# A delta-rule layer on Trainium2: half of the output projection done in two parts, around the state inputs

## What is computed

```python
def _L0_attn_a_ref(x, Wq, Wk, Wv, Wbeta, Wg1, Wg2, g_norm, Wo):
    h, hd = (Wbeta.shape[0], d // Wbeta.shape[0])        # 16 heads of 32
    q = silu(x @ Wq.T).reshape(b, n, h, hd)
    k = silu(x @ Wk.T).reshape(b, n, h, hd)
    v = (x @ Wv.T).reshape(b, n, h, hd)
    beta = 2.0 * jax.nn.sigmoid(x @ Wbeta.T)
    k = k * jax.lax.rsqrt(jnp.sum(k * k, axis=-1, keepdims=True) + EPS)
    o = _delta_rule(q, k, v, beta).reshape(b, n, d)      # S += k (beta (v - k S)); o = q S
    gate = jax.nn.sigmoid(x @ Wg1.T @ Wg2.T)
    og = (o * gate).reshape(b, n, h, hd)
    rms = jax.lax.rsqrt(jnp.mean(og * og, axis=-1, keepdims=True) + EPS)
    og = (og * rms).reshape(b, n, d) * g_norm
    return og @ Wo.T
x = x + _L0_attn_a_ref(_layernorm(x, axis=-1), ...)
```

## Time and profile before

| | us |
|---|---|
| median of 3 runs | 5043.79 |
| lowest, highest | 5043.69, 5046.62 |
| span of the profiled execution | 5045.7 |

### The profile page before, as it was taken

The page is one execution under the profiler, slowest core; times in us unless marked ns, Lnnn a source line. Parts: engine busy times, 40 slices in busy tenths (PEclk is TensorE's granted clock), DMA queues, the critical chain, the costliest instruction groups (busy, mean ns, idle before and its releaser), DMA issues.

```text
span 5045.7 us, 144755 instructions
## 1 busy us (share of the span) xinstructions
PE 4586.8 (91%) x63104; PEld 3211.9 (64%) x63104; DVE 3631.5 (72%) x7890; ACT 2410.3 (48%) x4592; POOL 716.4 (14%) x909
## 2 busy tenths in 40 slices
PE   5799999999999998499999999999999999999998
PEld 4677777777777776356546646655654664665564
DVE  3677666676776666287787788778778778877876
ACT  3244433333333333164564565466456457546545
POOL 0000000000000000012211211221221221122121
PEclk9899999999999998699999999999999999999999
DMA  2222222222222222100000000000000000000000
GB/s 62 49 70 69 72 62 62 62 62 62 62 69 63 62 66 62 64 1 18 2 18 18 18 2 18 18 1 18 18 2 18 18 10 10 18 18 2 18 9 10
DMA packets 352135, 171.77 MB, mean 34 GB/s; under 512 B 300016, under 2 KB 300784, under 8 KB 350736
## 3 DMA queue, kind: packets, MB, share of 16 engines
q1 hardware_dynamic: 342528, 145.20, 10.8%
q10 hardware_dynamic: 8976, 17.30, 1.2%
HBM read 93.74 MB, written 67.63 MB: 32 GB/s over the span
## 4 chain that ended last, share of the span: by engine, by line
PE 43%; DVE 11%; ACT 2%; issue 1%; DMA 1%; POOL 1%; SPq 0%; DVEq 0%; ACTq 0%; POOLq 0%
PE row_psum L1682 9%; PE row_psum L1707 9%; PE row_psum L40 5%; PE row_psum L42 5%; PE row_psum L41 5%; DVE smax L1963 5%; PE row_psum L1695 4%; PE row_psum L1755 1%; DVE xr_lo L1831 1%; PE row_psum L1735 1%; DVE probs L1943 1%; PE row_psum L1473 1%; DVE stats L1797 1%; POOL rstd L1276 1%; PE row_psum L1654 1%
## 5 line engine op out<-in xcount | busy, mean ns | idle before, releaser
L1963 DVE TENSOR_REDUCE smax<-row_psum 128x1 f32<-128x512 f32 x2048 | 1270.4, 681 | 96.9 <-PE row_psum L1682 93.3
L1405 ACT ACTIVATE probs<-row_psum 128x512 f32<-128x512 f32 x2048 | 1090.7, 603 | 349.8 <-PE row_psum L1695 329.7
L1682 PE MATMUL row_psum<-k_stack,q_stack 64*128 64x512 f32 (+1 forms) x2048 | 740.3, 440 | 50.6 <-DVE smax L1963 24.5
L1695 PE MATMUL row_psum<-q_stack,k_stack 64*128 64x512 f32 (+1 forms) x2048 | 733.1, 458 | 22.3 <-ACT probs L1405 9.1
L1682 PEld LDWEIGHTS row_psum<-k_stack,q_stack 64*128 64x128 f32 (+1 forms) x2048 | 354.3, 188 | 499.5 <-DVE smax L1963 367.7
L1707 PE MATMUL row_psum<-probs,v_aug 128*32 128x512 f32 x4096 | 538.9, 603 | 1.6 <-ACT av_sb L1421 0.4
L1695 PEld LDWEIGHTS row_psum<-q_stack,k_stack 64*128 64x128 f32 (+1 forms) x2048 | 319.3, 184 | 225.8 <-ACT probs L1405 156.0
L876 DVE TENSOR_TENSOR lane_t<-lane_t,lane_p 128x30 f32<-128x30 f32 (+14 forms) x960 | 318.3, 332 | 33.0
L40 PE MATMUL row_psum<-wf_hi,xr_hi 128*128 128x320 f32 (+1 forms) x1024 | 331.9, 324 | 3.2 <-DVE xr_lo L1831 3.2
L873 DVE TENSOR_TENSOR lane_p<-lane_t 128x30 f32<-128x30 f32 (+14 forms) x960 | 315.5, 329 | 23.5
L42 PE MATMUL row_psum<-wf_hi,xr_lo 128*128 128x320 f32 (+1 forms) x1024 | 318.9, 311 | 0.0
(11 more groups left out here) (215 smaller groups left out, 10123.8 us busy)
## 6 DMA issues: line engine op xcount, KB each, us to landing
x_sp<-in_x ACTq DMA_DIRECT2D x33, 512.0 KB, 4.0
tri_dram<-tri SPq DMA_DIRECT2D x256, 64.0 KB, 2.0
lane_t<-tri_dram SPq DMA_DIRECT2D x32, 512.0 KB, 4.6
inv_dram<-lane_t SPq DMA_DIRECT2D x32, 512.0 KB, 2.6
inv_b<-inv_dram SPq DMA_DIRECT2D x256, 64.0 KB, 2.3
x_res<-in_x SPq DMA_DIRECT2D x32, 512.0 KB, 3.8
x<-x_res SPq DMA_DIRECT2D x32, 512.0 KB, 3.7
xs<-x SPq DMA_DIRECT2D x16, 1024.0 KB, 5.6
```

Source lines behind the costliest of these rows:

```text
L1405: act.activation(probs[:, h % PROBS, tt, :], ps[:, m % STACK_BANKS, :], ACT.Exp, scale=float(DH) ** -0.5).then_inc(exp_ready, 1)
L1682: pe.matmul(ps[:, bank, :], q_stack[rows, qt, P * st:P * st + P], k_stack[rows, kv, :], start=True, stop=True).then_inc(max_mm, 1)
L1695: pe.matmul(ps[:, m % STACK_BANKS, :], k_stack[rows, kv, P * tt:P * tt + P], q_stack[rows, qt, :], start=True, stop=True).then_inc(score_m ...
L1963: dve.tensor_reduce(smax[:, g, st:st + 1], ps[:, bank_of("max", NT * g + st), :], AX.X, ALU.max).then_inc(max_ready, 1)
```

## The change

`output` gets an argument, the input blocks that it is to go through. Its waits are made on the first of them, and the projection is reported as done (`wo_mm`) after the last. TensorE calls it for the second tile with the first two input blocks before `state_inputs` and with the other two after. Both parts add up in bank BB. VectorE's `add_residual` for that tile moves from before the portion "inputs" of the inversion to behind `advance(0)`.

```diff
-            def output(b, s, t, further, ahead):
-
-                if further:
+            def output(b, s, t, further, ahead, inputs=range(KT)):
+
+                if further and inputs[0] == 0:
...
-                pe.wait_ge(ohi_ready, at(b, s, TS, t + 1))
-                pe.wait_ge(olo_ready, at(b, s, TS, t + 1))
-                for k in range(KT):
+                if inputs[0] == 0:
+                    pe.wait_ge(ohi_ready, at(b, s, TS, t + 1))
+                    pe.wait_ge(olo_ready, at(b, s, TS, t + 1))
+                for k in inputs:
...
-                last.then_inc(wo_mm, 1)
+                if inputs[-1] == KT - 1:
+                    last.then_inc(wo_mm, 1)
...
                 without_state(*now)
                 if behind:
-                    output(*behind, 1, further, ahead)
+                    output(*behind, 1, further, ahead, range(KT // 2))
                 state_inputs(*now)
+                if behind:
+                    output(*behind, 1, further, ahead, range(KT // 2, KT))
                 chain(*now, 0)
...
                 invert_ahead("transitions")
+                invert_ahead("inputs")
+                advance(*now, 0)
                 if behind:
                     add_residual(*behind, 1)
-                invert_ahead("inputs")
-                advance(*now, 0)
                 invert_ahead("chain0")
```

## The result

| | before | changed |
|---|---|---|
| median us (runs) | 5045.2 (4) | 5008.7 (4) |
| lowest, highest | 5043.69, 5057.3 | 5002.86, 5017.61 |
| span of the profiled execution | 5045.7 | 5008.0 |
| mean granted TensorE clock over the span | 0.963 | 0.973 |

The ratio is 0.9924 [0.9906, 0.9941], so the kernel became 0.8% faster, where 0.4% was forecast (5023 us; 5008.7 lies within 5003 to 5049). A second set of runs of the changed kernel gave 5004.06 us (6 runs) beside 5043.86 for the kernel before (21 runs), ratio 0.9924 [0.99, 0.9949].

What follows compares the result with a forecast made beforehand. TensorE was taken to be bound in the state chain by waits for 256-instruction program blocks. From the 5045.7 us span, +6 switches, -15 blocks, -12 clock gave 5024.7, with the span 1.9 above the median 5023 us; range 5003 to 5049.

Steps and rivals of the forecast that it cites:

- Blocks, -15 us: TensorE's program blocks: large matmuls moved to the next block cut stalls by about 0.5 us a step, over 31 steps.
- Step A: Step kind whose chain stall of 1.52 us goes while one of about 1.0 us appears in state_inputs: gain 0.5 us.
- Step B: Step kind with a 1.90 us stall inside the chain: gain between 0.05 and 1.05 us, in the middle 0.55.
- floor of 3.85 us: Least time from edge to edge assumed for a 256-instruction TensorE block that ends in a stall.
- Switches, +6 us: One more pair of switches between large and tiny matmuls on TensorE: +0.2 us a step, bounds 0 and +11.
- The clock, -12 us: TensorE's granted clock: a quarter of the lower-clock time goes, at 0.35 us per microsecond; bounds 0 and -25 us.
- VectorE's move worth nothing itself: An earlier state add on VectorE gains nothing, since TensorE's own key sums set the start of chain 1.
- cover of 0.9 us for 0.69: VectorE's slack before the second state add, 0.9 us, hides the moved 0.69 us add, so it costs nothing.
- (1): Rival: the stall only moves between blocks and the clock is untouched; median 5042 us, chance 0.27.
- the Trainium skill's rule: Block edges in TensorE's instruction fetch are mostly hidden, so only the switch term remains: 5050 us, chance 0.05.
- (2): Rival: TensorE's clock falls earlier, ahead of the chain; slower, 5056 to 5065 us for ten such steps, chance 0.09.
- (3): Rival: VectorE's slack before the second state add goes; 5052 us, chance 0.04.

Runs made afterwards that it cites:

- 0 / 4: The changed kernel with all twelve matmuls of the second projection behind state_inputs, none ahead: 5073.39 us, ratio 1.0057 to the kernel before.
- three-and-one split: The changed kernel with nine of the twelve projection matmuls ahead of state_inputs and three behind: 5019.97 us, ratio 0.9953 to the kernel before.
- VectorE's part alone: The kernel before with only VectorE's add_residual moved behind advance(0), TensorE's order unchanged: 5037.19 us, ratio 0.998.
- tiny filler: The changed kernel with 64 extra unused tiny matmuls (128 in the trace) behind state_inputs in 29 of 32 steps: 5138.41 us, ratio 1.0193.

## Why the prediction came out as it did

**What bounds the kernel there** was read rightly. The stalls in the chain are edges of program blocks: a block of tiny matmuls put in stalls once a step, large ones without use take stalls away, 3.84 and 3.85 us between edges came back in two other kernels, and nearly every stall ends 1.15 to 1.6 us behind a packet of the instruction queue.

**Blocks, -15 us.** All rows of issue fell by 15.1 us. The split was as forecast as well: 20.9 us left before L693 and L699 (about 20 forecast), and 14.2 before L682; with the rows of L40 to L42, 5.3 us for all large matmuls of these lines, that makes at most 19.5 (15 to 20 forecast). Step by step it was less good. Step A stalls 0.85 us in L682 (forecast 1.0) and not at all in the chain (forecast none), so it gained 1.52 - 0.85 = 0.67 us there (0.5 forecast), less 0.29 for a longer stall before L672 (0.71 for 0.42). Step B gained 1.90 - 0.45 = 1.45 us, above the 1.05 of the upper end: the block ahead of its stall, for which 0.5 to 1.0 us was put down, cost at most the 0.15 by which L682 is longer (1.44 for 1.29). What was wrong is the floor of 3.85 us applied to every block. Step A's block begins with a stall and takes 3.84 us. Step B's begins without one: 43 matmuls into L682, at about 1071.9, by the count of 128. It is worked off in 3.1 us, stalls 0.45 and so takes 3.5; its packet runs from 1073.12 to 1074.08, and TensorE goes on 1.38 us later, the same as behind other packets. The block ahead of it is worked off in 2.9 us without a stall; its packet starts some 0.8 us after the estimated edge, earlier than behind a stall. That an edge without a stall lets the next fetch start earlier is a reading of these rows, not tested by itself, and that queued matmuls are the cover, as the prediction has it, no row shows.

**Switches, +6 us.** The account leaves 7 and 8 us for the changed kernel, near the forecast, but the rest of kernels with as many switches as before (0 / 4: +11) is no smaller, so the term isn't confirmed by it. It lies within its bounds of 0 and 11.

**The clock, -12 us, is the term that was mis-sized.** A quarter of the lower-clock time was to go; from 300 to 1850 us two thirds went, 132 to 44 us. The mechanism was named (full-size matmuls between L682 and the chain, shorter stalls), and the count of long stalls, 14 to 2, goes with it; the price of 0.35 was near the 0.3 that fits, and the share was an estimate with no row behind it. 103 us less at 0.3 is 31 us, past the -25 given as the bound. With it in place of 12 the sum would have been 5045.7 + 6 - 15 - 31 = 5006, the span was 5008.0. So most of the gain comes from the clock, not from the stalls removed, two thirds of it by the account (31 of 46 us). The three-and-one split bears it out: 11.5 us fewer stalls, but only 62 of the 103 us at the lower level, and only 60% of the gain.

**VectorE's move worth nothing itself** held for the start of chain 1, shown by VectorE's part alone; the 0.2% of that kernel go with its clock. What the prediction didn't price is that the move is the condition of the other part: without it the state add waits for a projection that ends later, and the whole gain is lost. The prediction asked what the move may cost, and not what leaving it out would. The cover of 0.9 us for 0.69 held: the wait for the state occurs once, 1.1 us.

**The rivals.** (1) The stall moved in part, to L682, but in sum 15 us went, so it didn't only move. By the Trainium skill's rule the result would have been 5050 us; 5008.7 and the tiny filler speak against it here. (2) In the changed kernel one of the ten falls in 300 to 1850 us comes behind a stall in L682, so the clock didn't fall earlier there. In 0 / 4, which has twice the tiny matmuls in one run, it does: 17 of 30 falls come less than 4 us after the beginning of a stall in L682. Even so the clock is no lower than before as a whole (0.965), and that kernel is slower by its stalls. (3) VectorE's cover stayed.

**The range** reached down to 5003, it said with both gains at 1.5 times their size. That reason gives 5045.7 + 6 - 1.5 x 27 - 1.9 = 5009 only; 5003 takes the switches at nothing as well. The measured 5008.7 thus lies at the end of what the stated reason covers, and that it lies inside is in part luck: one term was 2.6 times its size, past its bound, and the range was wider than its reason.

## What to carry to other kernels

Where idle time of TensorE is put down to "issue" and its spots lie 256 instructions apart, spread large matmuls evenly among the tiny ones, so that no block is short: the place of twelve large matmuls was worth 0.8% here, and the best of five splits was the even one, with its neighbours 12 to 15 us behind. Count the granted clock in the same account, since fewer and shorter stalls brought back more there than in themselves (31 us beside 15 here, by the account). When an operation ends later through such a move, move its consumer too: in its engine's order it may stand ahead of something urgent.

## What the runs showed of the hardware

- A block of 256 instructions that was worked off faster took 3.47 us from edge to edge when it was all tiny matmuls and 3.84 or 3.85 us behind a stalled edge with large ones among them; a whole block of tiny matmuls put in cost 4.6 us a step, not the 1.6 of its busy time.
- Stalls between tiny matmuls ended 1.15 to 1.6 us after the end of a packet of the instruction queue (46 of 49, 47 of 51, 66 of 69 in three kernels), and the next packet started 1.1 to 1.7 us after that in three cases of four.
- Between runs of the same kernel, a microsecond more at the lower clock went with 0.3 us more of span (0.29 in 21 runs).
- 48.7 us of useless large matmuls made a kernel 0.3% faster.
- At the granted clock of 0.50 the state chain took 3.43 us from one to the next, against 1.90. TensorE had run tiny matmuls ahead of that fall, which came 1.6 us into a stall of 2.16 us.
